# Nine unit slots for x, stores and loads of x in shifted periods, and their issues regrouped behind the halo rows

## The chip, the cores and the metric

The kernel runs on one core of one Trainium2 chip. The metric is the device time of one execution in microseconds. All engines of the core work side by side: TensorE (PE, with its weight loads PEld), VectorE (DVE), ScalarE (ACT), GpSimd (POOL), and SyncE (SP), which here does nothing but issue DMAs.

## The reference

Two residual stages on x of shape (4, 96, 128, 128), float32. Group norm has 32 groups of 3 channels each. The first stage is a sum of depthwise 1x1, 3x3 and 5x5 convolutions, which the kernel folds into one 5x5 kernel for each channel. The second stage is one 3x3 kernel with a bias, the same for all channels.

```python
    def _L0_conv_ref(x, w1, w3, w5, alpha):
...
        out1 = _dwconv(x, w1, 0)
        out3 = _dwconv(x, w3, 1)
        out5 = _dwconv(x, w5, 2)
        return alpha[0] * x + alpha[1] * out1 + alpha[2] * out3 + alpha[3] * out5
...
    x = x + _L0_conv_ref(_gn(x), L0_conv_w1, L0_conv_w3, L0_conv_w5, L0_conv_alpha)
    x = x + _L1_conv_ref(_gn(x), L1_conv_w, L1_conv_b)
    return x
```

## The kernel before

**Units.** The work is cut into NU = 16 units. A unit is one group of 3 channels (CG) in the lower 64 partitions and another in the upper 64, for all NB = 4 images ("batches" below, b). A partition holds two neighbouring image rows. A unit of x is 1.5 MB, and so is a unit of the output.

**Periods.** The program runs over PERIODS = 18 periods j. In period j the first stage (called X) convolves unit j and the second stage (called Y) convolves unit j - 2. In the same period DVE takes the statistics of x of unit j + 2, adds the result of X's convolution to x (`evacuate`, L697), takes the statistics for Y and evacuates Y. ACT normalizes (L551, L552: a float32 copy and its fp16 rounding), POOL makes the fp16 remainder of both (`low_part`, L864), and PE multiplies by banded weight matrices (L377). A third of Y's result has to change partition halves: ACT copies it into `cross` (L561) and POOL adds it (`cross_add`, L873).

**Halo rows.** Rows at the border of a half are needed by the other half, shifted in several ways. They go through DRAM: `edges_out` writes the border rows of the normalized unit (L216 for X, four issues; L220 for Y, two issues), and `edges_in` waits until these have landed and reads them back, several times shifted, into `halo` (L236, four issues). PE multiplies them after the unit's bands. `load_band` reads the banded weights of the next unit (L303, three issues), `save_pair` writes the weights of a later pair of units to DRAM (L284, two issues, every second period).

**SP's order.** All of these are issued by SP in the order of the program, on one DMA queue, together with the bulk: `load_pair` (L250) loads two units of x at once, in eight issues of 384 KB, and `store_pair` (L263) stores two units of the output at once. An even period stores and an odd one loads. In a period SP issues Y's rows out, bands, (saved weights,) Y's rows in, bulk of batches 0 and 1, X's rows out, bulk of batch 2, X's rows in, bulk of batch 3:

```python
            for j in range(PERIODS):
...
                in_and_out(j, (0, 1))
                if j + 1 < NU:
                    edges_out(sp, X, j + 1)
                in_and_out(j, (2,))
                if j + 1 < NU:
                    edges_in(sp, X, j + 1)
                in_and_out(j, (3,))
```

`edges_in` holds up everything behind it on SP until the rows written by `edges_out` are in DRAM.

**Slots.** x lies in NX = 4 slots of two units each. The load of pair m waits for the store of pair m - 4. Units 0 to 3 are loaded ahead of the loop, units 4 and 5 in period 1, 6 and 7 in period 3, and so on up to 14 and 15 in period 11; DVE needs the first unit of a pair in the period after its load.

Of the kernel before, what the change touches and what calls it, by code (L numbers as in the profile page):

```python
# [5 lines left out]
def preact_conv_stack(nc: bass.Bass, x: bass.AP, w1: bass.AP, w3: bass.AP, w5: bass.AP, alpha: bass.AP,  # L6
# [15 lines left out]
    CG = C // GROUPS  # L22
# [16 lines left out]
    TAPS = (range(K5), range(1, K5 - 1))  # L39
    NX = 4  # L40
    NQ = NU + 3
# [12 lines left out]
    with ctx:  # L54
        def sb(name, shape, dt=fp32):
            return ctx.enter_context(nc.sbuf_tensor(name, shape, dt))
# [42 lines left out]

        cross = sb("cross", [P, NCROSS, NB, W])  # L100
        stats = sb("stats", [P, 2, 2, NB, 2, 6])
# [31 lines left out]
        x_unit_in = [sem(f"x_unit_in{n}") for n in range(1, 4)]  # L133
        x_in = [sem(f"x_in{r}") for r in range(NX)]
        band_in = [sem(f"band_in{p}") for p in range(2)]
        stored = [sem(f"stored{r}") for r in range(NX)]
        edges_landed = [sem(f"edges_landed{s}") for s in "XY"]
# [24 lines left out]
        def first_channel(i, g):  # L162

            return 4 * CG * (i // 2) + 2 * CG * g + CG * (i % 2)

        def x_of(i):

            return xt[:, (i // 2) % NX, :, i % 2, :, :, :]

# [21 lines left out]
        def crossed_to(i):  # L191

            return sum(crossed(n, c) for n in range(i + 1) for c in range(CG))

        def halo_landed(n):
# [44 lines left out]

        def load_unit(eng, n, b, done):
            for g in range(2):
                c = first_channel(n, g)
                eng.dma_start(xt[HALVES[g], (n // 2) % NX, b, n % 2, :, :, :].rearrange("p c e w -> p (c e) w"),  # L244
                              x[b, c:c + CG, :, :].rearrange("c (e p) w -> p (c e) w", e=2)).then_inc(done, 16)

        def load_pair(eng, m, b):
            for g in range(2):
                c = first_channel(2 * m, g)
                eng.dma_start(xt[HALVES[g], m % NX, b, :, :, :, :].rearrange("p u c e w -> p (u c e) w"),  # L250
                              x[b, c:c + 2 * CG, :, :].rearrange("c (e p) w -> p (c e) w", e=2)).then_inc(x_in[m % NX], 16)

        def store_unit(eng, n, b):
            for g in range(2):
                c = first_channel(n, g)
                eng.dma_start(out[b, c:c + CG, :, :].rearrange("c (e p) w -> p (c e) w", e=2),
                              xt[HALVES[g], (n // 2) % NX, b, n % 2, :, :, :].rearrange("p c e w -> p (c e) w"))\
                   .then_inc(stored[(n // 2) % NX], 16)

        def store_pair(eng, m, b):  # L260
            for g in range(2):
                c = first_channel(2 * m, g)
                eng.dma_start(out[b, c:c + 2 * CG, :, :].rearrange("c (e p) w -> p (c e) w", e=2),  # L263
                              xt[HALVES[g], m % NX, b, :, :, :, :].rearrange("p u c e w -> p (u c e) w"))\
                   .then_inc(stored[m % NX], 16)

        @block.sync
        def _(sp):
# [7 lines left out]
            for b in range(2, NB):  # L276
                load_unit(sp, 0, b, x_first_in[b])

# [32 lines left out]
            for b in range(NB):  # L311
                load_unit(sp, 1, b, x_unit_in[0])
            edges_out(sp, X, 0)
# [9 lines left out]
            for b in range(NB):  # L323
                load_unit(sp, 3, b, x_unit_in[2])

            def unit_ready(n):

                sp.wait_ge(evac_done[Y], CG * (n + 1))
                sp.wait_ge(cross_added, crossed_to(n))

            def in_and_out(j, batches):

                m = (j + 3) // 2 if j % 2 else j // 2 - LAG
                for b in batches:
                    if j % 2 and 2 <= m < NU // 2:
                        if m >= NX:
                            sp.wait_ge(stored[m % NX], 128 * (m // NX))
                        load_pair(sp, m, b)
                    elif j % 2 == 0 and m >= 0:
                        unit_ready(2 * m + 1)  # L340
                        store_pair(sp, m, b)
                    elif j == PERIODS - 1:
                        unit_ready(LAST - 1)
                        store_unit(sp, LAST - 1, b)

            for j in range(PERIODS):
                y = j - LAG
                if 0 <= y < LAST:
                    edges_out(sp, Y, y)
                if 1 <= j < LAST:  # L350
                    load_band(j + 1)
                if j % 2 == 0 and 2 <= j < NU - 2:
                    save_pair(j // 2 + 1, k_out)
                if 0 <= y < LAST:
                    edges_in(sp, Y, y)
                in_and_out(j, (0, 1))
                if j + 1 < NU:
                    edges_out(sp, X, j + 1)
                in_and_out(j, (2,))
                if j + 1 < NU:  # L360
                    edges_in(sp, X, j + 1)
                in_and_out(j, (3,))
            unit_ready(LAST)
            for b in (0, 1):
                store_unit(sp, LAST, b)
            for r in range(NX):
                sp.wait_ge(stored[r], 256 if r < NX - 1 else 384)

        @block.tensor
        def _(pe):  # L370
# [51 lines left out]
            def edge(s, i, c):  # L422

                if c == 0:
                    pe.wait_ge(halo_in[s][i % 2], halo_landed(i))

                def used(rows):
                    return slice(rows.start, rows.start + HROWS[s])

                tiles(s, c, lambda rows, half: halo_w[s][used(rows), CG * i + c, half, :] if s == X else halo_w[s][used(rows), half, :],  # L430
                      lambda rows, half: halo[s][used(rows), i % 2, :, c, 0:W], False, True)
# [18 lines left out]
            def halo_weights():  # L450
# [3 lines left out]
                for g, rows in enumerate(HALVES):  # L454
                    def of_half(t):
                        return t[:, 0:C].rearrange("k (m g u) -> k m g u", g=2, u=2 * CG)[:, :, g, :]
                    for q in range(4):
# [61 lines left out]
        def _(act):  # L519
# [3 lines left out]
            for b in range(2):  # L523
                load_unit(act, 0, b, x_first_in[b])
            act.wait_ge(const_ready, 3)
# [29 lines left out]
            def cross_over(i, c):  # L555

                act.wait_ge(conv_done[Y], 4 * CG * i + 4 * (c + 1))
                if i >= 1:
                    act.wait_ge(cross_added, NCROSS * (i - 1) + min(c, NCROSS - 1) + 1)
                for to, frm in ((LO, HI), (HI, LO)):  # L560
                    cr = nc.scalar.activation(cross[to, c, :, :].rearrange("p b w -> p (b w)"), ps[frm, c, 1, :], ACT.Identity,  # L561
                                              scale=unscale[frm, NU * CG:NU * CG + 1])
                cr.then_inc(cross_out, 1)

            def halo_weights():
# [5 lines left out]
                for q in range(4):  # L571
                    nc.scalar.copy(halo_w[X][:, :, (1, 1, 0, 0)[q], (0, 1, R - 2, R - 1)[q]], made[:, 0:NU * CG, q])\
                      .then_inc(halo_w_ready, 1)
# [8 lines left out]
            for b in range(NB):  # L582
                load_unit(act, 2, b, x_unit_in[1])
            root(1)
# [28 lines left out]
            for b in (2, 3):  # L613
                store_unit(act, LAST, b)

        @block.vector
        def _(dve):
# [12 lines left out]
            nc.vector.memset(stats[:, :, :, :, :, :], 0.0).then_inc(const_ready, 1)  # L630
            nc.vector.memset(halo_w[X][:, :, :, :], 0.0).then_inc(halo_w_zero, 1)
            nc.vector.memset(pick_x[:, :, :], 0.0).then_inc(picks_zero, 1)
# [93 lines left out]
            def x_stats(i, b):  # L726
                if i == 0:
                    dve.wait_ge(x_first_in[b], 32)
                elif i < 4:
                    if b == 0:  # L730
                        dve.wait_ge(x_unit_in[i - 1], 128)
                elif b == 0:
                    m = i // 2
                    dve.wait_ge(x_in[m % NX], 128 * (m // NX + (1 if m % NX >= 2 else 0)))
                return stats_of(X, i, b)
# [101 lines left out]
        def _(pool):  # L837
# [31 lines left out]
            def cross_add(i, c):  # L869

                pool.wait_ge(cross_out, crossed_to(i - 1) + sum(crossed(i, k) for k in range(c + 1)))
                here = x_of(i)[:, :, c, 1, :]
                nc.gpsimd.tensor_tensor(here, here, cross[:, c, :, :], ALU.add).then_inc(cross_added, 1)  # L873

# [76 lines left out]
```

## Time and profile before

| what | value |
|---|---|
| time, median of 3 runs | 430.67 us (428.61 to 430.91) |
| the profiled execution's own time | 432.64 us |
| its span (first to last instruction) | 430.8 us |
| PE busy | 318.5 us (74%) |
| DVE busy | 318.1 us (74%) |
| ACT busy | 304.1 us (71%) |
| POOL busy | 262.3 us (61%) |
| queue of SP, share of 16 DMA engines | 60.5% |
| bytes moved | 69.40 MB, mean 161 GB/s |

No engine is busy for more than three quarters of the span, so these shares alone don't name the bound. They are means over a head (to about 75 us), the periods that load and store x (about 127 to 335 us), the last periods without loads, and a tail. SP does not appear in the table, because issuing DMAs isn't counted as busy time; the timeline of SP has to be read for it.

### The profile page before, as it was taken

How to read it: one execution, taken by the hardware profiler on the slowest of the kernel's cores; microseconds unless marked ns; L12 is line 12 of the kernel's file. 1: busy time of each engine (PE TensorE's matmuls, PEld its weight loads, DVE VectorE, ACT ScalarE, POOL GpSimd, SP SyncE). 2: the span in 40 equal slices, each digit the busy share in tenths (PEclk: the TensorE clock that was granted, in tenths of full speed). 3: DMA queues.
4: the chain of work that ended last, by engine and by line, in shares of the span. 5: the costliest groups of instructions: out<-in, count | busy, mean ns of one | idle time of the engine just before them, and what ended most of it. 6: DMA issues, size and time to landing. Idle time of an engine off the chain costs nothing.

```text
span 430.8 us, 12547 instructions
## 1 busy us (share of the span) xinstructions
PE 318.5 (74%) x5206; PEld 276.8 (64%) x5206; DVE 318.1 (74%) x688; ACT 304.1 (71%) x372; POOL 262.3 (61%) x206
## 2 busy tenths in 40 slices
PE   2491586754986998679894998499848989898440
PEld 2361273643986798459883897389836989897220
DVE  7861899971886998399929994889649996779620
ACT  1407257089999699939995899759993999977320
POOL 6405055058788578827885588738882788865601
PEclk9997596995999899969996999889998999999685
DMA  6689488201687769676986788676868514731965
GB/s 151 169 174 204 129 188 169 73 3 41 159 200 164 199 177 210 158 189 202 199 194 171 198 184 202 161 214 173 189 163 223 145 41 118 201 97 28 264 173 146
DMA packets 112829, 69.40 MB, mean 161 GB/s; under 512 B 4540, under 2 KB 109892, under 8 KB 112772
## 3 DMA queue, kind: packets, MB, share of 16 engines
q1 hardware_dynamic: 106088, 65.31, 60.5%
q10 hardware_dynamic: 6684, 3.29, 3.3%
q8 instruction: 41, 0.67, 0.7%
q14 instruction: 16, 0.13, 0.1%
HBM read 41.10 MB, written 27.48 MB: 159 GB/s over the span
## 4 chain that ended last, share of the span: by engine, by line
DVE 33%; DMA 21%; SPq 13%; ACT 13%; PE 9%; issue 4%; ACTq 2%; POOL 2%; POOLq 0%; DVEq 0%
DVE xt L697 15%; DVE stats L641 13%; DMA xt<-in_x_dram 10%; PE ps L377 8%; DMA edge_scratch<-gnX 6%; ACT gn_f L551 5%; SPq L236 5%; ACT gnX L552 4%; ACT cross L561 3%; SPq L216 3%; DMA edge_scratch<-gnY 2%; SPq L250 2%; POOL gnX L864 1%; SPq L263 1%; ACTq L244 1%
## 5 line engine op out<-in xcount | busy, mean ns | idle before, releaser
L377 PE MATMUL ps<-gnX,band 64*64 64x512 f16 x2880 | 181.6, 397 | 29.9 <-DVE xt L697 18.1
L377 PEld LDWEIGHTS ps<-gnX,band 64*64 64x64 f16 x2880 | 161.1, 188 | 46.6 <-issue 40.2
L697 DVE SCALAR_TENSOR_TENSOR xt<-ps,unscale,xt 128x512 f32<-128x512 f32 (+1 forms) x194 | 143.8, 747 | 22.9 <-PE ps L377 20.1
L641 DVE BATCH_NORM_STATS2 stats<-xt 128x6 f32<-128x384 f32 x256 | 120.9, 546 | 45.6 <-DMA xt<-in_x_dram 44.9
L377 PE MATMUL ps<-gnY,band 64*64 64x512 f16 x1728 | 116.8, 414 | 33.7 <-DVE xt L697 33.7
L864 POOL TENSOR_TENSOR gnX<-gn_f,gnX 128x768 f16<-128x768 f32 x60 | 92.7, 1545 | 60.7 <-ACT gnX L552 60.7
L377 PEld LDWEIGHTS ps<-gnY,band 64*64 64x64 f16 x1728 | 97.9, 190 | 49.1 <-ACT gnY L552 23.0
L551 ACT ACTIVATE gn_f<-xt,g_add,g_mul 128x768 f32<-128x768 f32 x120 | 122.1, 1017 | 4.9 <-DVE g_add L681 4.3
L864 POOL TENSOR_TENSOR gnY<-gn_f,gnY 128x768 f16<-128x768 f32 x60 | 92.7, 1545 | 31.0 <-ACT gnY L552 31.0
L561 ACT ACTIVATE cross<-ps,unscale 64x512 f32<-64x512 f32 x94 | 64.2, 683 | 51.0 <-PE ps L377 49.4
L873 POOL TENSOR_TENSOR xt<-xt,cross 128x512 f32<-128x512 f32 x47 | 61.7, 1315 | 57.3 <-ACT cross L561 57.2
L552 ACT ACTIVATE gnX<-xt,g_add,g_mul 128x768 f16<-128x768 f32 x64 | 64.7, 1015 | 1.1 <-DVE g_add L681 1.1
L552 ACT ACTIVATE gnY<-xt,g_add,g_mul 128x768 f16<-128x768 f32 x64 | 64.7, 1015 | 0.0
L530 ACT ACTIVATE std<-var,eps_t 128x8 f32<-128x8 f32 x19 | 5.7, 301 | 54.6 <-DVE var L664 54.4
L439 PE MATMUL ps_s<-stats,ones_mean 64*64 64x32 f32 x76 | 5.8, 224 | 24.9 <-DVE stats L641 23.9
L377 PE MATMUL ps<-haloY,halo_wY 35*64 35x512 f16 x192 | 20.8, 391 | 3.8 <-DMA haloY<-edge_scratch 3.8
L439 PEld LDWEIGHTS ps_s<-stats,ones_mean 64*64 64x64 f32 x76 | 6.0, 142 | 26.9 <-issue 17.9
L377 PE MATMUL ps<-haloX,halo_wX 60*64 60x512 f16 x192 | 21.3, 394 | 2.4 <-DMA haloX<-edge_scratch 2.4
L648 DVE TENSOR_REDUCE ps_s<-ps_s 128x8 f32<-128x32 f32 x19 | 3.8, 198 | 14.9 <-PE ps_s L439 14.8
L377 PEld LDWEIGHTS ps<-haloY,halo_wY 35*64 35x64 f16 x192 | 8.9, 109 | 5.8 <-DMA haloY<-edge_scratch 4.2
L377 PEld LDWEIGHTS ps<-haloX,halo_wX 60*64 60x64 f16 x192 | 8.6, 108 | 4.3 <-DMA haloX<-edge_scratch 3.8
L666 DVE RECIPROCAL ps_s<-std 128x8 f32<-128x8 f32 x19 | 4.0, 211 | 9.8 <-ACT std L530 9.8
(78 smaller groups left out, 97.9 us busy)
## 6 DMA issues: line engine op xcount, KB each, us to landing
out_dram<-xt SPq DMA_DIRECT2D x56, 384.0 KB, 4.8
xt<-in_x_dram SPq DMA_DIRECT2D x48, 384.0 KB, 6.4
band<-diag_scratch SPq DMA_DIRECT2D x48, 160.0 KB, 3.0
haloX<-edge_scratch SPq DMA_DIRECT2D x32, 123.4 KB
xt<-in_x_dram SPq DMA_DIRECT2D x20, 192.0 KB, 4.3
xt<-in_x_dram ACTq DMA_DIRECT2D x12, 192.0 KB, 6.0
out_dram<-xt SPq DMA_DIRECT2D x12, 192.0 KB, 4.0
haloX<-edge_scratch SPq DMA_DIRECT2D x32, 61.7 KB
```

The lines of the kernel that those rows point to most:

```text
L216: eng.dma_start(edge_dram[s][p, g, :, side, :, :].rearrange("h r e -> r h e"), src).then_inc(edges_landed[s], 16)
L236: eng.dma_start(halo[s][R * g + at * n:R * g + (at + parts) * n, p, :, :, :] .rearrange("r b c w -> r (b c w)")[:, 0:EDGE], bass.AP(src.te ...
L250: eng.dma_start(xt[HALVES[g], m % NX, b, :, :, :, :].rearrange("p u c e w -> p (u c e) w"), x[b, c:c + 2 * CG, :, :].rearrange("c (e p) w ...
L377: mm = nc.tensor.matmul(ps[to, c, half, :], weights(rows, half), moving(rows, half), start=first, stop=last)
L439: nc.tensor.matmul(ps_s[rows, 0:8 * NB], ones_mean[rows, :], stats[rows, n % 2, :, :, :, :].rearrange("h s b e (d t) -> h (s b e d) t", d= ...
L551: nc.scalar.activation(gn_f[:, f_slot(s, i, b), :, :, :], src, ACT.Identity, **by)
L552: nc.scalar.activation(gn_hi[s][:, i % 2, :, b, :, PAD:PAD + W].rearrange("p e c w -> p c e w"), src, ACT.Identity, **by).then_inc(hi_done ...
L561: cr = nc.scalar.activation(cross[to, c, :, :].rearrange("p b w -> p (b w)"), ps[frm, c, 1, :], ACT.Identity, scale=unscale[frm, NU * CG:N ...
L641: st = nc.vector.bn_stats(stats[:, q_of(at, i) % 2, at, b, e, :], flat[:, SUB * e:SUB * (e + 1)])
L697: ev = nc.vector.scalar_tensor_tensor(out=here, in0=ps[frm, c, half, :].rearrange("h (b w) -> h b w", b=NB), scalar=unscale[rows, at:at + ...
L864: nc.gpsimd.tensor_tensor(gn_lo[s][:, i % 2, :, b, :, PAD:PAD + W].rearrange("p e c w -> p c e w"), gn_f[:, f_slot(s, i, b), :, :, :], gn_ ...
L873: nc.gpsimd.tensor_tensor(here, here, cross[:, c, :, :], ALU.add).then_inc(cross_added, 1)
```

## The change

Six things change.

1. x lies in NX = 9 slots of one unit, `xt[P, NB, NX, CG, 2, W]`, where it had 8 unit places in 4 pairs. Channels are dealt out differently (`first_channel`), so that any two neighbouring units are contiguous in DRAM.
2. Loads move a period ahead: units 4 and 5 in period 1 as before, 6 and 7 in period 2, 8 and 9 in period 4, up to 14 and 15 in period 10. Units 8 and 9 lie in the last and the first slot and are loaded apart, in issues of 192 KB.
3. Stores move to odd periods: unit 0 in period 3, units 1 and 2 in period 5, up to 11 and 12 in period 15, then 13, 14 and 15 one by one. A load waits for the store of its own batch alone.
4. SP's order within a period: bulk of batches 0 and 1 behind Y's rows in, as before; batches 2 and 3 both behind X's rows in. Nothing stands between X's rows out and X's rows in.
5. `cross` has two buffers in place of three. ACT's copy number k waits for POOL's add number k - 2 (k - 3 before).
6. The halo weights `halo_w[X]` overlap in memory, 66 columns apart where they had 128, which makes DVE's memset of them smaller.

```diff
-    NX = 4
+    NX = 9
+    PRE = 4
...
-        halo_w = [sb("halo_wX", [P, NU * CG, 2, R], fp16), sb("halo_wY", [P, 2, R], fp16)]
+        halo_w = [sb("halo_wX", [P, NU * CG * (R + FAR[0]) + R - FAR[0]], fp16), sb("halo_wY", [P, 2, R], fp16)]
...
-        xt = sb("xt", [P, NX, NB, 2, CG, 2, W])
+        xt = sb("xt", [P, NB, NX, CG, 2, W])
...
-        cross = sb("cross", [P, NCROSS, NB, W])
+        cross = sb("cross", [P, 2, NB, W])
...
-            return 4 * CG * (i // 2) + 2 * CG * g + CG * (i % 2)
+            return C // 2 * g + CG * i
...
+            def stores_in(j):
+
+                if j < LAG + 1:
+                    return None
+                if j == LAG + 1 or j >= NU:
+                    return j - LAG - 1, 1
+                return (j - LAG - 2, 2) if j % 2 else None
+
+            def loads_in(j):
+
+                if j == 1:
+                    return PRE
+                return j + PRE if j % 2 == 0 and 2 <= j < NU - PRE else None
...
             def in_and_out(j, batches):
 
-                m = (j + 3) // 2 if j % 2 else j // 2 - LAG
                 for b in batches:
-                    if j % 2 and 2 <= m < NU // 2:
-                        if m >= NX:
-                            sp.wait_ge(stored[m % NX], 128 * (m // NX))
-                        load_pair(sp, m, b)
-                    elif j % 2 == 0 and m >= 0:
-                        unit_ready(2 * m + 1)
-                        store_pair(sp, m, b)
-                    elif j == PERIODS - 1:
-                        unit_ready(LAST - 1)
-                        store_unit(sp, LAST - 1, b)
+                    if stores_in(j) is not None:
+                        n, units = stores_in(j)
+                        unit_ready(n + units - 1)
+                        store(sp, n, b, units)
+                    n = loads_in(j)
+                    if n is not None:
+                        if n + 1 >= NX:
+                            sp.wait_ge(stored[b], 32 * stores_until(n + 1 - NX))
+                        if joint(n):
+                            load(sp, n, b, 2, x_in[n // 2 % 2])
+                        else:
+                            for k in range(n, n + 2):
+                                load(sp, k, b, 1, x_in[n // 2 % 2])
...
                 in_and_out(j, (0, 1))
                 if j + 1 < NU:
                     edges_out(sp, X, j + 1)
-                in_and_out(j, (2,))
                 if j + 1 < NU:
                     edges_in(sp, X, j + 1)
-                in_and_out(j, (3,))
+                in_and_out(j, (2, 3))
...
-                if i >= 1:
-                    act.wait_ge(cross_added, NCROSS * (i - 1) + min(c, NCROSS - 1) + 1)
+                k = crosses_before(i, c)
+                if k >= 2:
+                    act.wait_ge(cross_added, k - 1)
```

**SP, where x is loaded.** In the kernel before, this is the loading part of an odd period and the start of the even one behind it. An issue with 64x12x128 moves two units of one batch and half; x4 are two batches.

```order
L250 DMA xt<-in_x_dram 64x12x128 x4
L216 DMA edge_scratch<-gnX 2x2x1584 x4
L250 DMA xt<-in_x_dram 64x12x128 x2
L236 DMA haloX<-edge_scratch 40x1x1580
L236 DMA haloX<-edge_scratch 20x1x1580
L236 DMA haloX<-edge_scratch 40x1x1580
L236 DMA haloX<-edge_scratch 20x1x1580
L250 DMA xt<-in_x_dram 64x12x128 x2
L220 DMA edge_scratch<-gnY 4x1x1584 x2
L303 DMA band<-diag_scratch 128x1x640 x3
L284 DMA diag_scratch<-diag 6x8x710 x2
```

In the changed kernel the loading part stands in an even period, and an odd one follows:

```order
L266 DMA xt<-in_x_dram 64x12x128 x4
L221 DMA edge_scratch<-gnX 2x2x1584 x4
L241 DMA haloX<-edge_scratch 40x1x1580
L241 DMA haloX<-edge_scratch 20x1x1580
L241 DMA haloX<-edge_scratch 40x1x1580
L241 DMA haloX<-edge_scratch 20x1x1580
L266 DMA xt<-in_x_dram 64x12x128 x4
L225 DMA edge_scratch<-gnY 4x1x1584 x2
L308 DMA band<-diag_scratch 128x1x640 x3
```

Four loads now stand directly ahead of Y's rows out (gnY), where two stood; the two loads between X's rows out and in are gone from there; and the saved weights no longer follow, so that only the bands stand between Y's rows out and Y's rows in.

**SP, where the output is stored.** In the kernel before, an even period and the start of the odd one behind it:

```order
L263 DMA out_dram<-xt 64x12x128 x4
L216 DMA edge_scratch<-gnX 2x2x1584 x4
L263 DMA out_dram<-xt 64x12x128 x2
L236 DMA haloX<-edge_scratch 40x1x1580
L236 DMA haloX<-edge_scratch 20x1x1580
L236 DMA haloX<-edge_scratch 40x1x1580
L236 DMA haloX<-edge_scratch 20x1x1580
L263 DMA out_dram<-xt 64x12x128 x2
L220 DMA edge_scratch<-gnY 4x1x1584 x2
L303 DMA band<-diag_scratch 128x1x640 x3
```

In the changed kernel, an odd period and the start of the even one:

```order
L270 DMA out_dram<-xt 64x12x128 x4
L221 DMA edge_scratch<-gnX 2x2x1584 x4
L241 DMA haloX<-edge_scratch 40x1x1580
L241 DMA haloX<-edge_scratch 20x1x1580
L241 DMA haloX<-edge_scratch 40x1x1580
L241 DMA haloX<-edge_scratch 20x1x1580
L270 DMA out_dram<-xt 64x12x128 x4
L225 DMA edge_scratch<-gnY 4x1x1584 x2
L308 DMA band<-diag_scratch 128x1x640 x3
L289 DMA diag_scratch<-diag 6x8x710 x2
```

Four stores now stand ahead of Y's rows out, and the saved weights have come in behind the bands.

## Rows read from the trace of the kernel before

**Rows 1.** Waits of DVE: who waited for what, us in total, times, longest us
```profile
DVE stats L641 <- DMA xt<-in_x_dram: 44.9, 7, 9.0
```

**Rows 2.** Chain that ended last, 295 to 320 us: start us, us, what
```profile
302.24 4.93 DMA edge_scratch<-gnX
...
310.70 7.27 DMA xt<-in_x_dram
```

**Rows 3.** SP issues in order of time: start us, us, line, op, tiles, count
```profile
247.98 2.65 SPq L236 DMA_DIRECT2D haloY<-edge_scratch  x4
250.68 3.02 SPq L250 DMA_DIRECT2D xt<-in_x_dram  x4
254.32 1.94 SPq L216 DMA_DIRECT2D edge_scratch<-gnX  x4
...
261.24 2.79 SPq L236 DMA_DIRECT2D haloX<-edge_scratch  x4
264.07 2.25 SPq L250 DMA_DIRECT2D xt<-in_x_dram  x2
266.41 1.15 SPq L220 DMA_DIRECT2D edge_scratch<-gnY  x2
...
269.84 1.59 SPq L284 DMA_DIRECT2D diag_scratch<-diag  x2
271.65 2.79 SPq L236 DMA_DIRECT2D haloY<-edge_scratch  x4
274.54 4.36 SPq L263 DMA_DIRECT2D out_dram<-xt  x4
279.00 2.42 SPq L216 DMA_DIRECT2D edge_scratch<-gnX  x4
281.51 1.30 SPq L263 DMA_DIRECT2D out_dram<-xt  x2
283.26 3.63 SPq L236 DMA_DIRECT2D haloX<-edge_scratch  x4
287.00 1.34 SPq L263 DMA_DIRECT2D out_dram<-xt  x2
289.46 1.73 SPq L220 DMA_DIRECT2D edge_scratch<-gnY  x2
291.29 1.86 SPq L303 DMA_DIRECT2D band<-diag_scratch  x3
293.44 2.66 SPq L236 DMA_DIRECT2D haloY<-edge_scratch  x4
```

**Rows 4.** SP issues again, periods 2 and 4: an empty ring, and a start
```profile
97.70 1.14 SPq L216 DMA_DIRECT2D edge_scratch<-gnX  x4
100.20 2.69 SPq L236 DMA_DIRECT2D haloX<-edge_scratch  x4
...
133.09 2.65 SPq L236 DMA_DIRECT2D haloY<-edge_scratch  x4
```

**Rows 5.** SP issues, period 12: the end of the four cycles
```profile
317.58 2.65 SPq L236 DMA_DIRECT2D haloY<-edge_scratch  x4
```

**Rows 6.** Busy us by engine (instructions), clock, DMA share, GB/s of two stretches
```profile
220.00:266.40 46.40, 37.80 (x652) 33.65 (x649) 36.18 (x76) 38.96 (x47) 32.29 (x22) 0.93 0.78 190
360.20:379.40 19.20, 17.74 (x324) 17.04 (x321) 14.35 (x30) 19.01 (x24) 15.81 (x12) 1.00 0.67 185
```

**Rows 7.** PE in order of time, period 12
```profile
329.59 0.40 PE L377 MATMUL ps<-haloY,halo_wY 35*64 35x512 f16 x4
```

**Rows 8.** ACT in order of time, period 10
```profile
289.50 1.39 ACT L561 ACTIVATE cross<-ps,unscale 64x512 f32<-64x512 f32 x2
```

**Rows 9.** POOL in order of time, period 10
```profile
285.85 1.29 POOL L873 TENSOR_TENSOR xt<-xt,cross 128x512 f32<-128x512 f32 x1 [6.51 <-ACT cross L561]
```

**Rows 10.** DVE in order of time, head of the kernel
```profile
2.96 2.62 DVE L631 MEMSET halo_wX<- 128x3072 uint32 x1 [0.59 <-issue]
```

**Rows 11.** ACT issues in order of time, last period
```profile
403.33 2.01 ACTq L220 DMA_DIRECT2D edge_scratch<-gnY  x2
```

More of the change, by code:

```diff
@@ L193, in crossed_to, with crosses_before @@
             return sum(crossed(n, c) for n in range(i + 1) for c in range(CG))
+        def crosses_before(i, c):
+            return crossed_to(i - 1) + sum(crossed(i, k) for k in range(c))
         def halo_landed(n):
@@ L239, in edges_in, with images, rows_of, joint @@
                        .then_inc(halo_in[s][p], 16)
-        def load_unit(eng, n, b, done):
+        def images(t, n, g, b, units):
+            c = first_channel(n, g)
+            return t[b, c:c + units * CG, :, :].rearrange("c (e p) w -> p (c e) w", e=2)
+        def rows_of(n, g, b, units):
+            at = n % NX
+            return xt[HALVES[g], b, at:at + units, :, :, :].rearrange("p u c e w -> p (u c e) w")
+        def joint(n):
+            return n % NX + 1 < NX
+        def loaded(n):
+            return sum(128 if joint(k) else 256 for k in range(PRE, n + 1, 2) if (k - n) % 4 == 0)
+        def load(eng, n, b, units, done):
             for g in range(2):
[L243 to L247, printed above, removed]
+                eng.dma_start(rows_of(n, g, b, units), images(x, n, g, b, units)).then_inc(done, 16)
+        def store(eng, n, b, units):
             for g in range(2):
[L249 to L265, printed above, removed]
+                eng.dma_start(images(out, n, g, b, units), rows_of(n, g, b, units)).then_inc(stored[b], 16)
         @block.sync
@@ L323, in _ @@
             for b in range(NB):
-                load_unit(sp, 3, b, x_unit_in[2])
+                load(sp, 3, b, 1, x_unit_in[2])
             def unit_ready(n):
@@ L523, in _ @@
             for b in range(2):
-                load_unit(act, 0, b, x_first_in[b])
+                load(act, 0, b, 1, x_first_in[b])
             act.wait_ge(const_ready, 3)
@@ L571, in halo_weights @@
                 for q in range(4):
-                    nc.scalar.copy(halo_w[X][:, :, (1, 1, 0, 0)[q], (0, 1, R - 2, R - 1)[q]], made[:, 0:NU * CG, q])\
+                    at = (R, R + 1, R - 2, R - 1)[q]
+                    nc.scalar.copy(halo_w[X][:, at:at + (R + FAR[X]) * (NU * CG - 1) + 1:R + FAR[X]], made[:, 0:NU * CG, q])\
                       .then_inc(halo_w_ready, 1)
@@ L582, in _ @@
             for b in range(NB):
-                load_unit(act, 2, b, x_unit_in[1])
+                load(act, 2, b, 1, x_unit_in[1])
             root(1)
@@ L613, in _ @@
             for b in (2, 3):
-                store_unit(act, LAST, b)
+                store(act, LAST, b, 1)
         @block.vector
@@ L869, in cross_add @@
             def cross_add(i, c):
-                pool.wait_ge(cross_out, crossed_to(i - 1) + sum(crossed(i, k) for k in range(c + 1)))
+                k = crosses_before(i, c)
+                pool.wait_ge(cross_out, k + 1)
                 here = x_of(i)[:, :, c, 1, :]
-                nc.gpsimd.tensor_tensor(here, here, cross[:, c, :, :], ALU.add).then_inc(cross_added, 1)
+                nc.gpsimd.tensor_tensor(here, here, cross[:, k % 2, :, :], ALU.add).then_inc(cross_added, 1)
             mid = diag[:, R - 1 - PAD:R + PAD, :][:, ::-1, :]
```

30 lines of the change are left out of this document (16 added, 14 removed).

## Prediction

> **What bounds the kernel now.** I read the waits first. DVE stands idle 44.9 us in 7 stretches for x to land [rows 1], and the chain that ended last runs through such a landing, behind border rows that land [rows 2]. That invites the reading "x comes too late, load it earlier". Then I read what a period costs. Late in the kernel, where nothing is loaded, a period takes 19.2 us with ACT busy for 19.01 of them; in the middle, two periods take 46.4 us, with ACT busy for 38.96, PE for 37.80 and DVE for 36.18 [rows 6]. So with x in time, ACT would set 19.2 us, and the middle costs about 4 us a period over that. Last I read SP from issue to issue, and that decides. From Y's rows in at 247.98 to the same issue two periods on at 293.44, SP issues almost without a gap [rows 3]. Its only long gap is a landing: X's rows out end at 256.26, two loads fill 1.3 us, and X's rows in start at 261.24. SP hardly waits for a compute engine anywhere in the 45.5 us. It is a queue that runs through its own program: issue times plus landings that it waits for itself. The bound is therefore SP's order, and DVE's waits for x are one of its effects. Four such cycles run from 133.09 to 317.58, 46.1 us each [rows 4, 5].
>
> **SP's cycle in four stretches.** Between the starts of the rows in [rows 3]:
> - A, Y in to X in, with four loads and X out ahead of the landing: 261.24 - 247.98 = 13.26 us.
> - B, X in to Y in, behind loads: 271.65 - 261.24 = 10.41.
> - C, Y in to X in, with four stores: 283.26 - 271.65 = 11.61.
> - D, X in to Y in, behind stores: 293.44 - 283.26 = 10.18.
>
> *A and C keep their contents*, apart from the two bulk issues under the landing. In A these hid nothing: SP waited on for 3.6 us behind them. In C the landing (end of X's rows out at 281.42, X in at 283.26) was 1.84 us with or without them. I leave both stretches as they are, which means that those two issues (1.3 us each time) must now stand elsewhere, in B and D.
>
> *B grows.* Now X's rows in (2.8 us) are followed by four loads, Y's rows out, only the bands, and the wait for Y's rows. How long does that landing take behind four loads? The nearest rows are A's own: from the end of Y's rows in (250.63) to the landing it took 10.6 us with four loads ahead. Against two loads: in B it took 7.6 us from the end of X's rows in (264.03) to 271.65. The saved weights and bands that covered part of it do not shorten it. So B becomes 2.8 + 10.6 = 13.4 at least; two loads more (0.79 MB at the 190 GB/s of rows 6, 4.1 us) would make 14.5. I take 13.8: +3.4, bounds +3.0 and +4.1.
>
> *D grows.* X's rows in cost 3.63 there with two stores just ahead, and 2.8 without. Then come four stores (4.36 as in C), Y's rows out (1.73 here; 1.94 for X's behind loads), bands 1.86, the saved weights 1.59, and about 0.6 of gaps: 2.8 + 4.4 + 1.9 + 1.9 + 1.6 + 0.6 = 13.2, so +3.0. The lower bound counts only what is added (two stores at 1.3, the saved weights 1.6) less the faster rows in and some relief in the queue, 1.2 + 1.1: +1.9. The upper one gives Y's rows out the 2.4 us of X's behind four stores: +3.7.
>
> Together a cycle costs g = 6.4 us more (4.9 to 7.8).
>
> **The Trainium skill beside this.** What rests on it is apart from the sum. Its page "DMA: Bandwidth & Descriptors" (section "Queues, rings and completion order") says that the DMAs of one issuing engine share one row of rings, whose descriptors are consumed in ring order. By that, small border rows issued behind bulk wait for the bulk. The trace agrees: X's rows land 1.36 us after their last issue with nothing ahead (98.84 to 100.20) and about 5 us behind four loads (256.26 to 261.24) [rows 3, 4]. The same page (section "Anatomy of one DMA") fits a DMA at about 2 us fixed plus bytes over 436 GB/s; by that alone Y's rows would be covered by the bands, which is the second rival.
>
> **Where the cycles act.** Up to period 2, SP has idle time, and the loads of units 6 and 7 fit there. In period 3 Y's rows in come at about 100.20 + 13.8 = 114.0 [rows 4], behind four loads; that period is paced by compute, as SP stood idle there until its rows out were made. Stores of one unit instead of two follow, and I put SP's start of period 4 0.6 us later than 133.09. Units 8 and 9 are loaded by 16 issues of 192 KB; at about 0.66 us each, half of 1.30 [rows 3], eight take 5.3 us, within the landing that SP waits for anyway. Four cycles later Y's rows in of period 12 start at 317.58 + 0.6 + 4g = 343.8. Loads have ended then, and period 12 has no bulk.
>
> **From SP to compute.** PE first needed these rows at 329.59 [rows 7], though they had landed at about 317.58 + 2.65 + 2 = 322.2: 7.4 us of slack. The slack is used up first: 0.6 + 25.6 - 7.4 = 18.8 us later for PE. DVE's waits for x go, but PE's waits for halo rows take their place, as SP hands out both. From there the periods run at ACT's pace as before.
>
> **The small parts.** The memset of 3072 words (2.62 us [rows 10]) shrinks to 1615, -1.2 us at the head, as the kernel weights wait behind it. In the tail ACT's Y rows out (2.01 us for two small issues [rows 11]) and their rows in stood beside eight paired stores of units 12 and 13; now fewer are in flight: -2, between 0 and -4. `cross` with two buffers: ACT starts the third copy at 289.50, POOL had ended the first add at 285.85 + 1.29 = 287.14 [rows 8, 9], so the new wait is met with 2.4 us to spare; without that cover up to 1.3 us a period. The new strides of x and of the halo weights keep the inner runs, and I cost them at nothing, as every instruction on x already stepped over other units between batches; no row prices the new step, and DVE, where most of them run, has 10 us in 46.4 to spare [rows 6].
>
> Sum: 0.6 + 4 x 6.4 - 7.4 - 1.2 - 2.0 = +15.6 us. The span 430.8 becomes 446.4; the profiled execution's own 432.64 becomes 448.2; and since that lies 1.97 above the median, the median becomes 446.3. In general: 430.7 - 10.0 + 4g. **Own range**: 440 (g = 4.9) to 453 (g = 7.8 and less relief in the tail).
>
> **Rivals.**
> - *SP's cycle does not grow, and compute is freed (faster).* If bulk moved from one place of SP's program to another costs only what it did there, g = 0. For it: the number of issues per pair is unchanged, and 44.9 us of DVE's waits go. Against it: the two issues stood under a landing, and Y's rows now have four loads ahead. It gives 430.7 - 10.0 = 420.7; it decides below g = 2.5, where the sum is zero. If SP kept ahead of ACT altogether, the floor of 19.2 us a period for eight periods would go towards 400. Chance 0.14.
> - *Y's rows land soon after their issue, whatever is ahead.* Then B is 2.8 + four loads 3.0 to 3.8 + 1.15 + 1.9 + 0.4 = 9.6 or so, 0.8 to 1.1 below now, and with D's +3.0 g = 1.9 to 2.2: 428.3 to 429.5. The 5 us in A speak against it. Chance 0.06. (The fixed cost in the Trainium skill's DMA page, above, would have it so.)
> - *Half the growth*, g about 3.5, because the ring drains faster once SP waits for it: 434.7. Chance 0.10.
> - *My forecast*, 0.70. Within it the sum also can run higher, if small stores and loads cost more issues than hidden.
>
> A measurement of this kernel can tell about 0.5%, 2.2 us, from no change. Faster by more: 0.17; within it: 0.06 (around g = 2.5); slower by more: 0.77. The range reaches from the faster rival to beyond my own upper bound: 421 to 455.
>
> **What the profile after would show.** DVE's waits for x gone from period 4 on; PE waiting for haloX and haloY instead. From one start of Y's rows in to the one two periods on, about 52.5 us instead of 46.1, in the periods up to 12. Y's rows in waiting some 4 us behind the bands in odd periods. Periods 13 to 15 at 19.2 us. I am wrong if two periods take under 48.6 us there, if Y's rows land within 2 us behind four loads, or if PE shows no wait for halo rows.

## The result and the profile after

The changed kernel takes 471.33 us (median of 4 runs, 469.54 to 474.86) beside 430.79 for the kernel before: 1.0959 times as long, with a 95% interval of 1.0883 to 1.1035. The forecast had the sign, at 446.3 us, and its range ended at 455. The span of the profiled execution is 469.7 us. In this document a time is the median of all runs of a kernel, and a ratio is taken over the undisturbed ones alone, so the two can differ by some tenths of a percent. DVE, ACT and POOL are busy for as long as before (316.7, 304.0 and 261.2 us): they compute the same and wait more. PE is busy for 333.5 us beside 318.5, at a mean granted clock of 0.870 beside 0.903; what part of the time that costs, no run separates.

The waits of the kernel after (engine, line, waited for: us in total, times, longest):

```profile
DVE xt L725 <- PE ps L401: 90.7, 35, 8.3
...
PE ps L401 <- DMA haloY<-edge_scratch: 40.3, 12, 5.6
...
PE ps L401 <- DMA haloX<-edge_scratch: 27.0, 8, 5.0
...
DVE stats L669 <- DMA xt<-in_x_dram: 17.1, 4, 8.8
```

DVE's wait for x has fallen from 44.9 us in 7 stretches [rows 1] to 17.1 in 4, as forecast. PE now waits 67.3 us for halo rows, and DVE 90.7 us for PE. SP's issues over one cycle, from Y's rows in of period 8 to those of period 10:

```profile
251.76 2.92 SPq L241 DMA_DIRECT2D haloY<-edge_scratch  x4
254.72 3.56 SPq L266 DMA_DIRECT2D xt<-in_x_dram  x4
258.38 2.86 SPq L221 DMA_DIRECT2D edge_scratch<-gnX  x4
266.73 2.79 SPq L241 DMA_DIRECT2D haloX<-edge_scratch  x4
269.56 4.88 SPq L266 DMA_DIRECT2D xt<-in_x_dram  x4
274.54 1.33 SPq L225 DMA_DIRECT2D edge_scratch<-gnY  x2
275.97 2.61 SPq L308 DMA_DIRECT2D band<-diag_scratch  x3
281.98 2.65 SPq L241 DMA_DIRECT2D haloY<-edge_scratch  x4
284.73 5.07 SPq L270 DMA_DIRECT2D out_dram<-xt  x4
289.91 3.05 SPq L221 DMA_DIRECT2D edge_scratch<-gnX  x4
294.75 2.81 SPq L241 DMA_DIRECT2D haloX<-edge_scratch  x4
...
309.72 2.88 SPq L241 DMA_DIRECT2D haloY<-edge_scratch  x4
```

These answer to [rows 3]. The landings under which SP stands idle are seen between rows. X's rows out end at 261.24 and X's rows in start at 266.73, behind four loads; the bands end at 278.58 and Y's rows in start at 281.98, where 0.2 us were left in the kernel before. The cycle is 309.72 - 251.76 = 57.96 us here; the four from 141.17 to 365.01 average 55.96, where the forecast had 52.5 and the kernel before 46.1 [rows 4, 5]. PE in that cycle (the idle time before a row stands in brackets):

```profile
272.86 1.07 PE L401 MATMUL ps<-haloX,halo_wX 60*64 60x512 f16 x8 [3.95 <-DMA haloX<-edge_scratch]
...
286.66 0.64 PE L401 MATMUL ps<-haloY,halo_wY 35*64 35x512 f16 x4 [4.34 <-DMA haloY<-edge_scratch]
```

One other row of the trace after belongs here. The first 20 us, in which both kernels issue the same loads in the same order (DMA share and GB/s are the last two columns):

```profile
0.00:20.00 20.00, 7.01 (x70) 6.26 (x70) 13.15 (x58) 3.67 (x6) 9.33 (x36) 1.00 0.71 153
```

The kernel before moved 153 GB/s there with a share of 0.63. The same bytes keep the DMA engines busy for 13% longer (0.71 against 0.63), before any of SP's new order has begun. The page says the same of the whole run: SP's queue moves 65.31 MB as before, at 60.4% of the 16 engines' time,

```profile
q1 hardware_dynamic: 106344, 65.31, 60.4%
```

which is 0.604 x 469.7 = 283.7 us against 0.605 x 430.8 = 260.6 before. Nothing in the forecast makes a transfer itself slower.

### The profile page after: what moved, and what is told of

The parts are those of the page before. It is cut to its first block, busy times and chain, and to the rows that moved or that the text cites. A ratio compares the mean times of both kernels' runs of the same rounds, so it can differ in the third digit from the quotient of the medians.

```text
span 469.7 us, 12568 instructions
## 1 busy us (share of the span) xinstructions
PE 333.5 (71%) x5206; PEld 268.7 (57%) x5206; DVE 316.7 (67%) x688; ACT 304.0 (65%) x372; POOL 261.2 (56%) x206
## 3 DMA queue, kind: packets, MB, share of 16 engines
q1 hardware_dynamic: 106344, 65.31, 60.4%
## 4 chain that ended last, share of the span: by engine, by line
SPq 43%; DMA 27%; ACT 12%; DVE 5%; PE 4%; issue 4%; POOL 2%; ACTq 2%; POOLq 0%
SPq L241 12%; SPq L270 9%; SPq L266 9%; DMA edge_scratch<-gnY 8%; DMA edge_scratch<-gnX 8%; DMA xt<-in_x_dram 6%; ACT gn_f L577 5%; SPq L225 4%; PE ps L401 4%; SPq L221 4%; DMA haloY<-edge_scratch 4%; ACT gnX L578 3%; SPq L308 2%; ACT cross L588 2%; SPq L289 2%
## 5 line engine op out<-in xcount | busy, mean ns | idle before, releaser
L725 DVE SCALAR_TENSOR_TENSOR xt<-ps,unscale,xt 128x512 f32<-128x512 f32 (+1 forms) x194 | 144.6, 748 | 93.1 <-PE ps L401 90.7
L401 PE MATMUL ps<-gnX,band 64*64 64x512 f16 x2880 | 188.4, 411 | 20.6 <-ACT cross L588 9.5
L401 PEld LDWEIGHTS ps<-gnX,band 64*64 64x64 f16 x2880 | 159.2, 190 | 45.7 <-issue 38.7
L669 DVE BATCH_NORM_STATS2 stats<-xt 128x6 f32<-128x384 f32 x256 | 120.9, 545 | 17.7 <-DMA xt<-in_x_dram 17.1
L901 POOL TENSOR_TENSOR xt<-xt,cross 128x512 f32<-128x512 f32 x47 | 60.3, 1283 | 90.9 <-ACT cross L588 90.7
L401 PEld LDWEIGHTS ps<-gnY,band 64*64 64x64 f16 x1728 | 92.0, 190 | 17.6 <-issue 9.6
L401 PE MATMUL ps<-haloY,halo_wY 35*64 35x512 f16 x192 | 20.6, 459 | 40.3 <-DMA haloY<-edge_scratch 40.3
L401 PEld LDWEIGHTS ps<-haloY,halo_wY 35*64 35x64 f16 x192 | 7.2, 125 | 49.8 <-DMA haloY<-edge_scratch 45.7
L465 PEld LDWEIGHTS ps_s<-stats,ones_mean 64*64 64x64 f32 x76 | 6.0, 157 | 34.6 <-issue 24.4
L401 PEld LDWEIGHTS ps<-haloX,halo_wX 60*64 60x64 f16 x192 | 6.7, 113 | 31.1 <-DMA haloX<-edge_scratch 30.5
L676 DVE TENSOR_REDUCE ps_s<-ps_s 128x8 f32<-128x32 f32 x19 | 3.7, 195 | 13.3 <-PE ps_s L465 13.2
```

The source lines that it names most:

```text
L401: mm = nc.tensor.matmul(ps[to, c, half, :], weights(rows, half), moving(rows, half), start=first, stop=last)
L669: st = nc.vector.bn_stats(stats[:, q_of(at, i) % 2, at, b, e, :], flat[:, SUB * e:SUB * (e + 1)])
L725: ev = nc.vector.scalar_tensor_tensor(out=here, in0=ps[frm, c, half, :].rearrange("h (b w) -> h b w", b=NB), scalar=unscale[rows, at:at + ...
L901: nc.gpsimd.tensor_tensor(here, here, cross[:, k % 2, :, :], ALU.add).then_inc(cross_added, 1)
```

## The experiments

Theory O was that SP's order explains all of it and that slow packets follow from bulk four in a row; theory L that memory layout has a share of its own. "Packets" in the expectations are the 512 B packets of x and out; their mean time, from the packet records, is 33.9 ns before and 37.4 ns after.

**e1_after_old_order**: the changed kernel with SP's old grouping.

```diff
                 in_and_out(j, (0, 1))
                 if j + 1 < NU:
                     edges_out(sp, X, j + 1)
+                in_and_out(j, (2,))
                 if j + 1 < NU:
                     edges_in(sp, X, j + 1)
-                in_and_out(j, (2, 3))
+                in_and_out(j, (3,))
```

> The changed kernel with one line group put back: batch 2 again between X's rows out and X's rows in, batch 3 behind them. Theory O (the order of SP's issues is the whole cause; the slower 512 B packets of the trace after are an effect of the bulk standing four in a row): most of the 40 us comes back, 430 to 438 us, and mean time of a bulk packet falls back. Theory L (order and memory layout each have a share; the packets are slower from the first load on, where the order is the same): 448 to 458 us, and SP's two-period cycle is about 50 us, between 46.1 and 56.0.

447.58 us, ratio 1.0369 (1.0308 to 1.0429); SP's cycle is 51.6 us and the packets stay slow, 37.8 ns. Theory O falls: some 24 us are the order, and 17 are left. Theory L comes within half a microsecond of its range, with a longer cycle than it said.

**e2_before_new_order**: the kernel before with the same three lines the other way round.

> The kernel before with the one regrouping: nothing between X's rows out and in, batches 2 and 3 behind X's rows in. Theory O: 460 to 472 us. Theory L: the working of the prediction without the layout, 440 to 448 us, with a cycle of about 50 to 52 us in periods 4 to 12.

452.23 us, ratio 1.0448 (1.0364 to 1.0531). Its profile is that of the slowest of its four runs (456.10): cycle 51.1 us, packets 34.0 ns. Four issues in a row don't slow packets, and the order alone costs 21 us: O's 460 is missed, and L's 448 too, by 4.

**e3_before_new_channels** and **e4_before_batch_outermost**: two parts of the layout, each alone.

```diff
-            return 4 * CG * (i // 2) + 2 * CG * g + CG * (i % 2)
+            return C // 2 * g + CG * i
...
-        xt = sb("xt", [P, NX, NB, 2, CG, 2, W])
+        xt = sb("xt", [P, NB, NX, 2, CG, 2, W])
```

> The kernel before with the new dealing of channels alone (the two halves of a unit 48 channels, 3 MiB, apart in DRAM instead of 6). Theory O: 430.7 us, no change. Theory L with the cause in DRAM: bulk landings some 15% slower, 438 to 450 us. Theory L with the cause in SBUF: no change here.

> The kernel before with the batch as the outermost index of x in SBUF, as in the changed kernel (24 KB between batches of one unit instead of 6). Theory O: 430.7 us, no change. Theory L with the cause in SBUF: 438 to 450 us, bulk landings slower from the first load on. Theory L with the cause in DRAM: no change here.

429.33 us, ratio 0.9982 (0.9945 to 1.0019), and 430.00 us, ratio 0.9923 (0.9872 to 0.9973). Neither costs anything. The ratio under 1 with the batch outermost leans on one run of 423.58 us; the medians are 0.2% apart (430.00 and 431.01). Both guesses of theory L at the cause were wrong. What was left was where x begins. The halo weights lie ahead of x in SBUF; packing them (change 6) moved the start of x from byte 43520 of a partition, a multiple of 512, to 37696, which is 64 past a multiple of 256. No view of the profile shows an address, so the two starts are not shown. The step between them is, by the diff: `halo_wX` took 12,288 bytes of a partition and takes 6,460, and with its end rounded to 6,464 x moves by 5,824, which is 22 x 256 + 192. Theory P is that this slows the packets; theory M says that the shifted loads meet more traffic.

**e5_after_aligned**, and in the kernel before **e6_before_off_320** and **e8_before_off_256**: one unused tensor ahead of x, of 96, 160 and 128 elements of 2 bytes.

```diff
+        spare = sb("spare", [P, 96], fp16)
         xt = sb("xt", [P, NB, NX, CG, 2, W])
```

> The changed kernel with 192 unused bytes a partition ahead of x, so that x begins in SBUF at a multiple of 512 bytes again (37888), as in the kernel before (43520); in the changed kernel it begins at 37696, 64 bytes past a multiple of 256, because the halo weights ahead of it were packed. Theory P (the place of x slows every bulk packet, from the first load on): 512 B packets fall from 37.4 to about 34 ns and the time from 471 to about 450, what is left being the order. Theory M (earlier loads that meet more traffic, or small joint effects of the shifted periods, slow the packets): no change, 471.

> The kernel before with 320 unused bytes ahead of x: x begins at 43840, 64 bytes past a multiple of 256, as in the changed kernel, and nothing else moves in the program. Theory P: bulk packets at 37 to 40 ns, 440 to 452 us. Theory M: 431 us, no change.

> The kernel before with 256 unused bytes ahead of x: x begins at 43776, a multiple of 256 that is none of 512. If a multiple of 256 is enough: 431 us and packets as before. If it takes 512, the packet size: as with 320 bytes, 440 to 452 us. Theory M: 431.

e5: 445.27 us, 26 less than the changed kernel, ratio to the kernel before 1.0399 (1.0315 to 1.0482). e6: 455.49 us, ratio 1.0633 (1.0550 to 1.0716), from nothing but 320 unused bytes, and 3.5 us over the range of theory P. e8: 430.43 us, ratio 1.0028 (0.9990 to 1.0066). Theory P holds in both kernels, theory M falls, and a multiple of 256 is enough. The three agree with the two starts given above: 192 bytes more take the changed kernel's x to a multiple of 256, 320 take the other's off one, and 256 leave it on one.

The unused tensor moves everything that lies behind x as well, the normalized rows too, which DMAs read. The packet records tell the two apart. SP's queue needs 30 us more in e6 than in e8 (below), and 27.5 of them are the 512 B packets of x and out: 92,160 packets on that queue at 38.34 against 33.56 ns, over 16 engines. The first 20 us of e5 have the changed kernel's share at a higher rate (171 against 153 GB/s):

```profile
0.00:20.00 20.00, 7.01 (x70) 6.27 (x70) 14.14 (x58) 4.66 (x7) 10.34 (x36) 1.00 0.71 171
```

and SP's queue needs 0.586 x 443.0 = 259.6 us:

```profile
q1 hardware_dynamic: 106344, 65.31, 58.6%
```

The pages of e6 and e8 (queue; stores and loads of 384 KB with the median us from issue to landing):

```profile
q1 hardware_dynamic: 106088, 65.31, 63.6%
...
out_dram<-xt SPq DMA_DIRECT2D x56, 384.0 KB, 5.2
xt<-in_x_dram SPq DMA_DIRECT2D x48, 384.0 KB, 7.3
```

```profile
q1 hardware_dynamic: 106088, 65.31, 59.8%
...
out_dram<-xt SPq DMA_DIRECT2D x56, 384.0 KB, 4.8
xt<-in_x_dram SPq DMA_DIRECT2D x48, 384.0 KB, 6.3
```

e6's queue needs 0.636 x 452.2 = 287.6 us, e8's 0.598 x 430.8 = 257.6. Loads, which write x into SBUF, land in 7.3 us instead of 6.3; stores, which read it, in 5.2 instead of 4.8. These medians hold the time in the queue as well as the transfer. In e6 DVE's wait for x is 68.9 us.

**e7_after_aligned_old_order**: both causes taken out; left are nine slots, the shifted periods and two cross buffers.

> The changed kernel with x at a multiple of 512 and with the old order (batch 2 between X's rows out and in, batch 3 behind). What is left of the change is nine slots, the shifted periods and two cross buffers. Theory P: both causes gone, 431 us or less, as loads come a period earlier and DVE has no wait for x: 422 to 433. Theory M: as with the old order alone, 447.

422.16 us (four runs: 415.22, 421.55, 422.78 and 423.09) beside 429.40: faster than the kernel before in every run, whose lowest of 13 is 426.35. By how much stays loose, 7 us by the medians and 14 by the lowest run, and there is no interval for this ratio. The profile is that of the run of 423.09, at a cycle of 47.5 us. The cycle is no shorter than before. What has gone is DVE's wait for x, 9.6 us in all against 44.9:

```profile
DVE stats L671 <- DMA xt<-in_x_dram: 9.6, 3, 7.7
```

The time is gained late: Y's rows in of period 12 start 2.6 us later than in the kernel before, and from there to the end of the span it takes 101.1 us against 113.2.

**e9_bulk_behind_x_out**, **e10_last_batch_behind_y_out**, **e11_one_batch_at_each**: three other orders on e7. The diff is e10's.

```diff
                 if 0 <= y < LAST:
                     edges_out(sp, Y, y)
+                if j:
+                    in_and_out(j - 1, (3,))
...
                 if j + 1 < NU:
                     edges_in(sp, X, j + 1)
-                in_and_out(j, (3,))
+                if j == PERIODS - 1:
+                    in_and_out(j, (3,))
```

> The changed kernel, aligned, with X's rows out ahead of all bulk of the period: batches 0 and 1 between X's rows out and X's rows in, 2 and 3 behind X's rows in. Theory Q (SP's own program with its landings sets the cycle): X's rows land within 2 us and under the issue of four transfers, some 9 us less a cycle in A and C; but SP then stands idle until POOL has made X's rows, and halo X is read behind four loads. If the first outweighs: 410 to 420 us. Rival R (compute's latency from POOL to halo X sets the period, so that bulk ahead of the halo reads costs what it saves): 425 to 440.

> The changed kernel, aligned, with the old order but batch 3 moved from behind X's rows in to behind the next period's Y rows out, so that one batch stands ahead of Y's rows and one fills their landing. Theory Q: the 10.6 us from X's rows in to the landing of Y's rows shrink by about 2 us after loads: 412 to 420 us against 422. Rival R: no change, 422.

> The changed kernel, aligned, with one batch of bulk at each of four places: behind Y's rows in, between X's rows out and in, behind X's rows in, and behind the next period's Y rows out. Theory Q: every landing has one batch ahead of it and is covered by one issue pair or more; SP's cycle comes near the pure issue time of about 40 us: 405 to 418 us. Rival R: 418 to 425.

e9: 442.62 us, ratio 1.0271 (1.0202 to 1.0340). e10: 415.49 us, ratio 0.9647 (0.9604 to 0.9691). e11: 417.61 us, ratio 0.9708 (0.9663 to 0.9752). The last two are in theory Q's ranges, though e11's cycle is 44.9 us and not near 40. Against the kernel before both are clearly faster. Against e7 they are 5 to 7 us faster by the medians, and e7's run of 415.22 lies within e10's four (413.69 to 415.87); that the order gains on e7 rests on the other three runs of e7 and on the cycle, 45.0 against 47.5. In e10, SP from X's rows in to Y's rows in, behind loads:

```profile
238.77 2.77 SPq L242 DMA_DIRECT2D haloX<-edge_scratch  x4
241.64 1.08 SPq L226 DMA_DIRECT2D edge_scratch<-gnY  x2
242.77 1.36 SPq L267 DMA_DIRECT2D xt<-in_x_dram  x2
244.22 1.87 SPq L309 DMA_DIRECT2D band<-diag_scratch  x3
246.19 2.64 SPq L242 DMA_DIRECT2D haloY<-edge_scratch  x4
```

From X's rows in to Y's rows in it takes 7.4 us where the kernel before took 10.4 (stretch B): Y's rows out go straight behind X's rows in, with one batch of bulk (two loads) fewer ahead, and these two loads and the bands fill their landing. e9 lies outside both ranges, theory Q's and rival R's:

```profile
272.07 4.05 SPq L242 DMA_DIRECT2D haloX<-edge_scratch  x4
...
291.13 3.53 SPq L267 DMA_DIRECT2D xt<-in_x_dram  x4
294.76 3.62 SPq L242 DMA_DIRECT2D haloX<-edge_scratch  x4
```

X's rows land in time, but the issues of the rows in now stall behind bulk (3.62 and 4.05 us for four, 2.77 in e10), and PE waits 35.5 us for Y's halo rows; its cycle is 49.3 us.

**e12_before_last_batch_moved**: e10's diff on the kernel before.

> The kernel before with one move: batch 3 from behind X's rows in to behind the next period's Y rows out. If SP's order alone is the limit, it gains what the same move gave the aligned changed kernel (422 to 415.5, some 6 us): 424 us. If the wait of DVE for x of the next unit is a limit of its own, which only the earlier loads remove, batch 3 now lands about 1.2 us later in every second period, and the time stays at 428 to 433 us.

446.32 us, ratio 1.0420 (1.0346 to 1.0495), slower than either expectation. DVE's wait for x:

```profile
DVE stats L644 <- DMA xt<-in_x_dram: 56.9, 8, 9.2
```

56.9 us against 44.9 [rows 1]. SP does gain behind the loads, where X in to Y in takes 9.1 us (224.21 to 233.27). Behind the stores it loses more, since it now stands idle for Y's rows to be made. SP, POOL, and SP again:

```profile
245.56 3.80 SPq L236 DMA_DIRECT2D haloX<-edge_scratch  x4
...
250.90 1.54 POOL L867 TENSOR_TENSOR gnY<-gn_f,gnY 128x768 f16<-128x768 f32 x1 [0.76 <-ACT gnY L555]
...
252.47 1.09 SPq L220 DMA_DIRECT2D edge_scratch<-gnY  x2
```

POOL ends at 252.44, after SP has been idle for 3.1 us. In the kernel before, POOL ends at 289.44, 2.6 us after SP's X rows in, but SP has two stores to issue meanwhile; Y's rows out start at 289.46 [rows 3].

```profile
287.89 1.55 POOL L864 TENSOR_TENSOR gnY<-gn_f,gnY 128x768 f16<-128x768 f32 x1 [0.75 <-ACT gnY L552]
```

So in the kernel before two limits lie close together, SP's own program and the compute that makes Y's rows. I read the second as late because DVE waits for x; no run separates that from other causes. A move that helps SP alone need not gain, then. In the profiled run of e12 (442.66 us, 10.0 over that of the kernel before) 4.4 us are lost before period 4 starts and 1.6 in each cycle. The other three runs are 2.5 to 5 us longer than that, for which there is no profile.

The times, where SP starts Y's rows in of periods 4 and 12, and a quarter of what lies between (SP's cycle):

| kernel | us | period 4 | period 12 | cycle, us | worked out, us |
|---|---|---|---|---|---|
| before | 430.79 | 133.09 | 317.58 | 46.1 | |
| after | 471.33 | 141.17 | 365.01 | 56.0 | 467.5 |
| e1 | 447.58 | 134.27 | 340.63 | 51.6 | 443.1 |
| e5 | 445.27 | 133.26 | 341.25 | 52.0 | 443.8 |
| e7 | 422.16 | 130.27 | 320.18 | 47.5 | 422.7 |
| e9 | 442.62 | 140.35 | 337.71 | 49.3 | 440.2 |
| e10 | 415.49 | 133.49 | 313.65 | 45.0 | 416.2 |
| e11 | 417.61 | 133.80 | 313.41 | 44.9 | 415.9 |

The last column is the forecast's own formula with the measured starts put in. Start and cycles together are the delay of period 12 against 317.58, so it reads 430.7 - 10.6 + (period 12 - 317.58). For the seven kernels with early loads it is within 4.5 us of the time. (The measured starts hold the shorter memset already, which the constant takes off once more; with -9.4 in place of -10.6 the seven lie within 3.3 us.) It does not hold where loads are late. From Y's rows in of period 12 to the end of the span the kernel before takes 113.2 us, e2 114.0, e6 111.4 and e12 112.6; the seven take 100.3 to 104.9. With early loads the rest of the kernel is 8 to 13 us shorter.

## Why the prediction was right about the order and missed a second cause

**The bound of the changed kernel was named rightly.** DVE's waits for x went and PE's for halo rows came, as said; the order alone costs 23 us there (e5 against e7) and 21 in the kernel before (e2). For the kernel before, the sentence that DVE's waits for x are one of the effects of SP's order goes too far: in e12 SP stands idle for Y's rows to be made, while DVE waits for x longer than before. The rival that SP's cycle does not grow when bulk is moved is refuted by e5, where g is 5.9. Its figure without growth, 420.7 us, is near what e7 takes (422.16), but e7 leaves the bulk where it was.

**The order was sized rightly.** Its stretches are seen in e5, where x begins at a multiple of 512:

```profile
264.01 2.65 SPq L242 DMA_DIRECT2D haloY<-edge_scratch  x4
...
275.85 2.81 SPq L242 DMA_DIRECT2D haloX<-edge_scratch  x4
...
289.03 2.87 SPq L242 DMA_DIRECT2D haloY<-edge_scratch  x4
```

The means of the four cycles of e5, and of the changed kernel:

| stretch | before | forecast | e5, aligned | after |
|---|---|---|---|---|
| A, Y in to X in, loads | 13.26 | 13.26 | 13.1 | 14.2 |
| B, X in to Y in, behind loads | 10.41 | 13.8 | 13.5 | 15.0 |
| C, Y in to X in, stores | 11.61 | 11.61 | 12.2 | 12.4 |
| D, X in to Y in, behind stores | 10.18 | 13.2 | 13.2 | 14.3 |

The first column is the one cycle that the forecast used [rows 3]. Over its four cycles the kernel before takes 13.3, 10.6, 12.1 and 10.1 us, so that C has not grown in e5 either, and g is 2.9 in B and 3.1 in D. B and D are within 0.3 us of the forecast, and e5's 445.27 us is 1 us from the forecast's 446.3. In part that is luck, since two things in the head that I had not foreseen nearly cancel. DVE in e5 starts on units 2 and 4 thus:

```profile
34.67 3.78 DVE L670 BATCH_NORM_STATS2 stats<-xt 128x6 f32<-128x384 f32 x8 [2.13 <-DMA xt<-in_x_dram]
...
75.88 3.78 DVE L670 BATCH_NORM_STATS2 stats<-xt 128x6 f32<-128x384 f32 x8 [4.88 <-DMA xt<-in_x_dram]
```

In e5 unit 2 is there at 34.67, where DVE of the kernel before waited for it until 42.8 us: with the head 1 to 2 us earlier, ACT's loads of unit 2 land before the stream of unit 3 from SP's queue gets in among them, as I read it. No run tested that by itself, but the 14 profiles line up with it. In e5, e9, e10 and e11 ACT's loads start 10.3 us or more ahead of SP's for unit 3, and DVE begins unit 2 at 34.6 to 36.6 us; in the other ten the lead is 9.9 us or less, and DVE begins at 40.3 to 44.3. e7, with x at a multiple of 512 as in e5, is one of the ten:

```profile
40.83 3.78 DVE L671 BATCH_NORM_STATS2 stats<-xt 128x6 f32<-128x384 f32 x8 [7.72 <-DMA xt<-in_x_dram]
```

So this gain doesn't follow from the place of x alone. Against it stand 4.88 us in period 2, for batches 2 and 3 of unit 4, which the new order sends behind X's rows in. In period 2 the kernel before has no such wait.

One bound was summed wrongly on the way. The lower one of D, +1.9, takes two stores at 1.3 us each, where [rows 3] has 1.30 to 1.34 for the pair; with 1.3 for both it is +0.6. And no row shows the 2 us for the landing of Y's rows in, on which the slack of 7.4 us rests. What the runs show is the whole from that start to the end: 113.2 us in the kernel before, less the 10.6 of the forecast, is 102.6, and the seven kernels take 100.3 to 104.9.

**The step that failed** is the term for the layout, put at nothing in one clause among the small parts: "The new strides of x and of the halo weights keep the inner runs, and I cost them at nothing". The strides of x do cost nothing (e4, and e3 for the channels). But the packed halo weights also move the tensor behind them, and with x off a 256-byte boundary each 512 B packet takes longer, 37.4 ns against 33.4 in e5. I costed that edit only as a shorter memset, and that term was right:

```profile
2.65 1.40 DVE L659 MEMSET halo_wX<- 128x1615 uint32 x1 [0.29 <-issue]
```

1.40 us instead of 2.62 [rows 10]. The same edit cost 26.1 us (471.33 - 445.27) through the address of x. It slows A, which was to stay as it was, by about 1 us, and B and D by 1.1 to 1.5, together 4.0 us a cycle, 16 in all; and the head is later. The same two starts of DVE in the changed kernel:

```profile
42.94 3.78 DVE L669 BATCH_NORM_STATS2 stats<-xt 128x6 f32<-128x384 f32 x8 [8.84 <-DMA xt<-in_x_dram]
...
82.63 3.77 DVE L669 BATCH_NORM_STATS2 stats<-xt 128x6 f32<-128x384 f32 x8 [5.07 <-DMA xt<-in_x_dram]
```

Unit 2 is late again, unit 4 as well, and period 4 starts 7.9 us later than in e5. Sixteen and 7.9 make 23.8 of the 26.1 us; the rest I have not traced. How much of the 7.9 us the place of x causes directly is open: with the old order unit 2 is late on either side, and period 4 starts 4.0 us later off the boundary (134.27 in e1, 130.27 in e7).

A rule bears on it that I had not weighed. The Trainium skill's page "DMA: Bandwidth & Descriptors" (section "How a descriptor splits into AXI transactions") says that a transaction must start at a 256-byte boundary, and that a descriptor which starts off one also pays for the bytes between the boundary and its start. Worked out from that, as an estimate, a descriptor of 512 B that starts 64 bytes past a boundary takes three transactions in place of two. e6 against e8 agrees with the boundary: 64 bytes past a multiple of 256 it is 455.49 us, at a multiple of 256 but not of 512 it is 430.43. The number of transactions no trace here shows.

**The other rivals.** Y's rows do not land soon whatever is ahead: behind four loads they took 3.4 us beyond the bands. The prediction sets a fit of the Trainium skill's page "DMA: Bandwidth & Descriptors" (section "Anatomy of one DMA") beside this rival; the page gives that fit for DMAs that GpSimd issues, and these are SP's. Half the growth did not come either (5.9 us a cycle in e5, where the rival had 3.5). No run has the two buffers for `cross` alone; in the changed kernel ACT waits nowhere for POOL.

## What to carry to other kernels

Where one engine issues all DMAs and also waits for some of them, add up its own program, issue times and landings, before believing any wait of a compute engine; a small transfer that is waited for should have little bulk ahead of it and some issues behind it. Then look for a second limit close behind: the move that shortened the cycle in e10 lengthened it in e12. And when a buffer's size changes, look at the addresses of everything allocated behind it: a saving in one tensor can take another off the boundary at which its DMAs are fast. The best kernel here by its median (e10, 415.49 us) keeps the nine slots and the early loads, starts x at a multiple of 512, and puts the last batch behind Y's rows out.

## What the runs showed that I had not expected

- With x 64 bytes past a multiple of 256 in SBUF, the DMA engines need 9 to 12% more time for the same 65.31 MB (283.7 against 259.6 us in the changed kernel, 287.6 against 257.6 in the kernel before), and loads into SBUF suffer more than stores out of it (7.3 against 6.3 us to landing, and 5.2 against 4.8, in e6 and e8).
- Issues of SP stall behind bulk in the queue: four rows-in issues that take 2.8 us with a drained queue take 3.6 to 4.1 with four bulk transfers just ahead (e9).
- From Y's rows in of period 12, when no more loads come, kernels with early loads need some 10 us less to the end than those with late ones (e7 101.1 us, before 113.2).
